# Rows transposed unscaled in the attention half, the inverse root moved behind the projection, and the side work placed at other ticks

## What is computed

```python
h = _layernorm(x) * (1 + ca) + sa
# for a in (global, local), with norm_w[a]:
hn = h * rsqrt(mean(h * h) + 1e-6) * norm_w[a]        # rmsnorm
q, k, v = split_heads(hn @ wq), ...                    # 16 heads of 8 for q, 4 for k and v
q, k = rope(q), rope(k)
q = q * rsqrt(mean(q * q) + 1e-6); k = ...             # qk_norm, per head
o = softmax(q @ k.T / sqrt(8), masked) @ v
h = h + merge_heads(o) @ wo
# then
x = x + ga * h
```

## Time and profile before

| | |
|---|---|
| median of 3 runs | 1370.69 us (1365.3 to 1371.41) |
| the profiled execution | 1370.85 us |
| its span | 1369.1 us |
| PE busy | 1176.2 us, 86% |
| DVE busy | 987.5 us, 72% |
| ACT busy | 821.8 us, 60% |
| POOL busy | 437.6 us, 32% |
| exponentials L742 | 384, 355.8 us |

### The profile page before, as it was taken

One profiled execution on the slowest core, in us unless ns is written; L12 is line 12 of the kernel. 1 busy time (PEld: TensorE's weight loads), 2 busy tenths in 40 slices (PEclk: granted clock), 3 DMA queues, 4 the chain that ended last, 5 costly groups with the idle time before them and its releaser, 6 DMA issues.

```text
span 1369.1 us, 36780 instructions
## 1 busy us (share of the span) xinstructions
PE 1176.2 (86%) x15602; PEld 698.9 (51%) x15602; DVE 987.5 (72%) x1573; ACT 821.8 (60%) x1218; POOL 437.6 (32%) x577
## 2 busy tenths in 40 slices
PE   3268888789888887867899999999999999999986
PEld 2123334344434554535566666666666666666653
DVE  4836765759575866869578777877778777877755
ACT  2179878788786664533555556455655566555641
POOL 1203030201013443665453333333433333333410
PEclk8579999999999998988899999999999999999997
DMA  3011302021021333110021011011110110111101
GB/s 97 5 38 44 124 29 85 18 92 32 17 94 32 125 109 109 48 45 18 17 76 26 21 26 26 21 25 26 29 26 22 25 26 22 27 24 26 29 6 62
DMA packets 37330, 59.79 MB, mean 44 GB/s; under 512 B 6416, under 2 KB 12464, under 8 KB 37168
## 3 DMA queue, kind: packets, MB, share of 16 engines
q1 hardware_dynamic: 37168, 57.44, 14.4%
HBM read 22.58 MB, written 16.78 MB: 29 GB/s over the span
## 4 chain that ended last, share of the span: by engine, by line
PE 46%; DVE 5%; issue 2%; ACT 1%; POOL 1%; DVEq 0%; POOLq 0%; ACTq 0%
PE psum L1229 8%; PE psum L1365 7%; PE psum L1318 5%; PE psum L1249 4%; PE psum L1340 4%; PE psum L1304 4%; PE psum L1239 4%; PE psum L1391 3%; DVE ffn_neg_max L1714 2%; PE psum L1289 1%; PE psum L1326 1%; PE psum L1295 1%; ACT ffn_hn L1570 1%; PE psum L1357 1%; PE psum L1261 1%
## 5 line engine op out<-in xcount | busy, mean ns | idle before, releaser
L742 ACT ACTIVATE att_probs<-psum 128x1024 f32<-128x1024 f32 (+2 forms) x384 | 355.8, 993 | 128.9 <-PE psum L586 127.3
L1661 POOL TENSOR_TENSOR ffn_rot<-ffn_rot,ffn_rot_sin 128x512 f32<-128x512 f32 x128 | 160.3, 1274 | 385.6 <-DVE ffn_rot L1692 385.6
L630 PE MATMUL psum<-att_probs,att_v 128*32 128x256 f32 (+3 forms) x3712 | 205.4, 349 | 2.2 <-DVE att_probs L905 1.3
L586 PE MATMUL psum<-att_q_stack,att_k_parts 64*128 64x512 bf16 (+4 forms) x1280 | 143.5, 299 | 43.6 <-ACT att_probs L742 28.6
L905 DVE TENSOR_TENSOR att_probs<-att_probs,att_causal_mask 128x1024 f32<-128x1024 f32 (+1 forms) x80 | 85.0, 1066 | 87.9 <-ACT att_probs L742 87.9
L630 PEld LDWEIGHTS psum<-att_probs,att_v 128*32 128x32 f32 x3712 | 97.0, 112 | 69.3 <-issue 40.5
L586 PEld LDWEIGHTS psum<-att_q_stack,att_k_parts 64*128 64x128 bf16 x1280 | 44.3, 95 | 146.4 <-ACT att_probs L742 88.6
L1543 ACT ACTIVATE ffn_max_t<-psum 68x128 bf16<-68x128 bf16 x64 | 17.4, 273 | 152.2 <-PE psum L1277 152.0
L1550 ACT ACTIVATE ffn_probs<-psum 128x1024 f32<-128x1024 f32 x64 | 65.6, 1025 | 59.2 <-PE psum L1304 59.2
L1512 ACT ACTIVATE ffn_sq<-psum 128x512 f32<-128x512 f32 x128 | 75.3, 594 | 27.9 <-PE psum L1229 27.7
L489 POOL TENSOR_TENSOR att_probs<-att_probs,att_local_mask 128x480 f32<-128x480 f32 (+1 forms) x48 | 61.9, 1295 | 79.9 <-ACT att_probs L742 79.8
(11 more groups left out here) (217 smaller groups left out, 2497.0 us busy)
## 6 DMA issues: line engine op xcount, KB each, us to landing
ffn_v_back<-ffn_v SPq DMA_DIRECT2D x120, 130.0 KB, 2.4
att_q_stack<-q_rows SPq DMA_DIRECT2D x28, 512.0 KB, 3.6
q_rows<-att_q_high SPq DMA_DIRECT2D x21, 256.0 KB, 4.5
q_rows<-att_q_mid SPq DMA_DIRECT2D x21, 256.0 KB, 4.2
q_rows<-att_q_low SPq DMA_DIRECT2D x14, 256.0 KB, 4.2
xres<-in_hidden SPq DMA_DIRECT2D x4, 512.0 KB, 4.3
out<-ffn_qk_t SPq DMA_DIRECT2D x3, 512.0 KB, 3.2
att_q_stack<-att_q_high SPq DMA_DIRECT2D x24, 32.0 KB, 2.0
```

Of the source, the lines that this page charges most:

```text
L586: ins = T.matmul(psum[:, banks[i] + at:banks[i] + at + width], k_parts[rows, p % 3, j, kt * P:(kt + 1) * P], q_stack[rows, turn % 2, j, q0 ...
L630: ins = T.matmul(psum[32 * g:32 * g + V_PAD, (4 + cc) * BANK + lo - cc * BANK: (4 + cc) * BANK + hi - cc * BANK], v[:, p % 4, kt, g, shift ...
L742: act.activation(probs[:, n % E_BUFS, 2 * j:2 * j + 2, 0:width], ps2((step % 2) * 2).rearrange("p (h c) -> p h c", h=2)[:, :, 0:width], AC ...
L1661: steps.did(pool.tensor_tensor(out, out, halves(k.rot_sin[:, n % 2, :])[:, :, 1 - half, :], ALU.add), g["added"] if half else None)
```

## The change

The rows are transposed as they are, and no longer wait for their inverse root; `scale` is gone. As q and k are normalised per head afterwards, an unscaled row changes only the weight of the epsilon: the head's epsilon becomes `eps_row`, the row's mean square (with its epsilon) times 1e-6. The values alone are multiplied by the inverse root, by DVE in the new steps `scale0` and `scale1`, which replace ACT's value copies. `refine` is the Newton step of the root alone. The tables of steps are shorter, there is one more (`CLOSE`, for phase 6), and nearly all ticks are other ones.

```diff
-LN_AT = (-14, -8, 10, 36)
-QKV_AT = (-10, -1, 25, 50, 75, 100, 125, 153)
-OUT_AT = ((23, 44, 47, 50), (70, 75, 94, 97), (100, 118, 120, 122), (144, 147, 149, 151),
-          (165, 167, 169, 176), (178, 180, 182, 184), (186, 190, 192, 194))
-POST_AT = (177, 186)
+LN_AT = (-14, -5, 19, 24)
+QKV_AT = (-12, 8, 34, 60, 85, 110, 135, 158)
+OUT_AT = ((23, 41, 63, 67), (72, 88, 92, 97), (100, 113, 117, 121), (129, 147, 149, 151),
+          (164, 166, 173, 175), (177, 179, 181, 183), (185, 189, 191, 193))
+POST_AT = (176, 184)
...
-RELAXED = dict(square=0, reduce=3, roots=6, scale=7, transpose=10, evacuate=11, project0=13, copy0=14, project1=16, copy1=17,
-               head_square=17, cos=18, head_reduce=20, head_roots=22, sin=21, newton=22, add=22, rotate=26, k_split=27,
-               q_transpose=29, q_hi=30, q_lo=31, k_transpose=33, k_hi=34, k_lo=34)
...
+RELAXED = dict(square=0, transpose=1, evacuate=2, reduce=3, roots=4, refine=4, project0=5, copy0=6, scale0=7,
+               project1=9, copy1=10, scale1=11, head_square=10, cos=11, head_reduce=13, sin=14, head_roots=14, newton=14,
+               add=15, rotate=18, k_split=19, q_transpose=21, q_hi=22, q_lo=23, k_transpose=24, k_hi=25, k_lo=25)
+FIRST = dict(square=0, transpose=0, reduce=0, evacuate=1, roots=1, refine=1, project0=2, project1=2, copy0=3, scale0=3,
+             copy1=3, scale1=3, head_square=3, cos=3, head_reduce=3, head_roots=4, sin=4, add=4, newton=4, rotate=4,
+             q_transpose=5, q_hi=5, k_split=5, q_lo=6, k_transpose=6, k_hi=6, k_lo=6)
+CLOSE = dict(square=0, transpose=1, evacuate=2, reduce=3, roots=4, refine=4, project0=4, copy0=5, scale0=6,
+             project1=7, copy1=8, scale1=9, head_square=8, cos=9, head_reduce=11, sin=12, head_roots=12, newton=12,
+             add=13, rotate=16, k_split=17, q_transpose=18, q_hi=19, q_lo=20, k_transpose=21, k_hi=22, k_lo=22)
+LAST = dict(square=0, transpose=0, evacuate=1, reduce=1, roots=2, refine=2, project0=2, copy0=2, scale0=3,
+            project1=4, copy1=4, scale1=5, head_square=4, cos=5, head_reduce=5, sin=6, head_roots=6, add=7, newton=7,
+            rotate=8, k_split=8, q_transpose=10, q_hi=11, q_lo=12, k_transpose=13, k_hi=14, k_lo=14)
...
-MODULATE_AT = -8
+MODULATE_AT = -10
...
                         if share[1]:
                             wait_side_free("transpose", p)
-                            pe.wait_ge(xr_ready, p + 1)
-                        transposes(side, nrm, share, xrt_in_psum)
+                            if a == 0:
+                                pe.wait_ge(h_ready, b + 1)
+                            else:
+                                pe.wait_ge(h_added, PHASES.index((0, b)) + 1)
+                        transposes(side, h[:, b], share, ht_in_psum)
...
                         c.did(act.activation(qk[:, tiles], src[:, :, 0:QK_COLS], ACT.Copy), qk_copied)
-                        c.did(act.activation(v_dims[:, p % 4, tiles],
-                                             src[:, :, QK_COLS:QKV_COLS].rearrange("p t (g d) -> p t g d", g=KV_HEADS),
-                                             ACT.Copy), v_ready)
...
+                for i in range(2):
+                    for p in qkv_due(("scale0", "scale1")[i], n):
+                        tiles = slice(i * TILES // 2, (i + 1) * TILES // 2)
+                        src = side_of(p, ("project0", "project1")[i]).rearrange("p (t c) -> p t c", t=TILES // 2)
+                        dve.wait_ge(qk_copied, 2 * p + i + 1)
+                        if p >= 4 and i == 0:
+                            dve.wait_ge(pv_done, last_unit[GROUP * (p - 4) + GROUP - 1] + 1)
+                        c.did(V.tensor_tensor(v_dims[:, p % 4, tiles],
+                                              src[:, :, QK_COLS:QKV_COLS].rearrange("p t (g d) -> p t g d", g=KV_HEADS),
+                                              widen(rstd[:, tiles].rearrange("p (t o u) -> p t o u", o=1, u=1),
+                                                    [P, TILES // 2, KV_HEADS, HEAD_DIM]), ALU.mult), v_ready)
...
                     c.did(V.tensor_scalar(row_sq[:], row_sq[:], 1.0 / D, ATT_EPS, ALU.mult, ALU.add), row_sq_ready)
-                for p in qkv_due("scale", n):
-                    a, b = PHASES[p]
+                    c.settle()
+                    c.did(V.tensor_scalar(eps_row[:], row_sq[:], ATT_EPS, None, ALU.mult))
+                for p in qkv_due("refine", n):
                     refine_root(row_turn["qkv", p])
-                    c.did(V.tensor_tensor(nrm[:], h[:, b], widen(rstd[:].rearrange("p (t o) -> p t o", o=1), [P, TILES, D]),
-                                          ALU.mult), xr_ready)
...
-                    c.did(V.tensor_scalar(mean_sq[:], mean_sq[:], 1.0 / HEAD_DIM, ATT_EPS, ALU.mult, ALU.add), mean_sq_ready)
+                    c.did(V.scalar_tensor_tensor(mean_sq[:], mean_sq[:], 1.0 / HEAD_DIM,
+                                                 widen(eps_row[:].rearrange("p (t o) -> p t o", o=1), [P, TILES, QK_HEADS]),
+                                                 ALU.mult, ALU.add), mean_sq_ready)
```

More of the change, by code:

```diff
@@ L247 @@
-FIRST = dict(square=0, reduce=0, roots=1, scale=1, transpose=2, evacuate=2, project0=3, copy0=3, project1=3, copy1=3,
-             head_square=4, cos=4, head_reduce=4, sin=5, add=5, head_roots=5, newton=5, rotate=5, k_split=5,
-             q_transpose=6, q_hi=6, q_lo=6, k_transpose=6, k_hi=6, k_lo=6)
-LAST = dict(square=0, reduce=1, roots=2, scale=3, transpose=7, evacuate=8, project0=9, copy0=9, project1=11, copy1=11,
-            head_square=11, cos=12, head_reduce=12, sin=13, add=14, head_roots=14, newton=15, rotate=16, k_split=16,
-            q_transpose=18, q_hi=19, q_lo=20, k_transpose=21, k_hi=22, k_lo=22)
@@ L254 @@
+LAST = dict(square=0, transpose=0, evacuate=1, reduce=1, roots=2, refine=2, project0=2, copy0=2, scale0=3,
+            project1=4, copy1=4, scale1=5, head_square=4, cos=5, head_reduce=5, sin=6, head_roots=6, add=7, newton=7,
+            rotate=8, k_split=8, q_transpose=10, q_hi=11, q_lo=12, k_transpose=13, k_hi=14, k_lo=14)
+QKV_STEPS = (FIRST,) + (RELAXED,) * (len(PHASES) - 3) + (CLOSE, LAST)
 URGENT = (0, len(PHASES) - 1)
@@ L336, in attention_stream @@
     mean_sq, root, rnorm, refine = (sb(n, [P, TILES, QK_HEADS]) for n in ("mean_sq", "root", "rnorm", "refine"))
+    eps_row = sb("eps_row", [P, TILES])
     stats, mv, mod = tail.stats, tail.mv, tail.mod
@@ L351, in attention_stream @@
     normed, h_ready, h_added = sem("normed"), sem("h_ready"), sem("h_added")
-    sq_ready, xr_ready, xrt_in_psum, ht_ready = sem("sq_ready"), sem("xr_ready"), sem("xrt_in_psum"), sem("ht_ready")
+    sq_ready, ht_in_psum, ht_ready = sem("sq_ready"), sem("ht_in_psum"), sem("ht_ready")
     qkv_in_psum, qk_copied, v_ready = sem("qkv_in_psum"), sem("qk_copied"), sem("v_ready")
@@ L498, in _ @@
                     if p not in URGENT:
-                        pool.wait_ge(xrt_in_psum, p)
+                        pool.wait_ge(row_sq_ready, row_turn["qkv", p - 1] + 1)
                         if a == 0:
@@ L646, in _ @@
                         share = share_of(qkv_tick(p, "transpose"), n, j, TILES)
+                        a, b = PHASES[p]
                         if share[1]:
                             wait_side_free("transpose", p)
-                            pe.wait_ge(xr_ready, p + 1)
-                        transposes(side, nrm, share, xrt_in_psum)
+                            if a == 0:
[3 more added lines that the diff above has]
+                        transposes(side, h[:, b], share, ht_in_psum)
                     for i in range(2):
@@ L756, in _ @@
                         if p:
-                            act.wait_ge(xrt_in_psum, p)
+                            act.wait_ge(row_sq_ready, row_turn["qkv", p - 1] + 1)
                         if a == 0:
@@ L770, in _ @@
                             act.wait_ge(head_sq_ready, p)
-                        if p >= 4 and i == 0:
-                            act.wait_ge(pv_done, last_unit[GROUP * (p - 4) + GROUP - 1] + 1)
                         c.did(act.activation(qk[:, tiles], src[:, :, 0:QK_COLS], ACT.Copy), qk_copied)
-                        c.did(act.activation(v_dims[:, p % 4, tiles],
-                                             src[:, :, QK_COLS:QKV_COLS].rearrange("p t (g d) -> p t g d", g=KV_HEADS),
-                                             ACT.Copy), v_ready)
                 for p in qkv_due("head_square", n):
@@ L860, in _ @@
                         dve.wait_ge(kt_in_psum, p)
-                    dve.wait_ge(xrt_in_psum, p + 1)
+                    dve.wait_ge(ht_in_psum, p + 1)
                     for i in range(2):
```

3 lines of the change are left out of this document (removed).

## The result

The changed kernel takes 1381.13 us in the median of four runs (1380.42 to 1381.33), the kernel before 1369.6 beside it. The ratio is 1.0079, with a 95% interval of 1.006 to 1.0098: slower by 0.8%, where 1366 was forecast. The profiled spans are 1379.3 and 1369.1 us.

The account below looks back on a forecast made before the run. ACT (84%) and PE (85%) were taken as near the bound in the global units. From 1370.85 us, start -14.1, waits going -20.1, waits coming +37.1, local units -6 and end -1.5 gave -4.6: 1366, range 1350 to 1384.

Parts of the forecast that it names:

- The start: Before the first score: transposes follow h directly, first score at 61.3 us, 14.1 us earlier, bounds 10 to 16.
- Phase 1: Ticks 19 to 31: layernorms of batches 2 and 3 moved into phase 1's DVE chain; waits of +15 us, bounds 6 and 20.
- piled up: Rival: head-root waits cost 4.5 us each, phase 1 its upper 20, POOL stands against DVE, small waits bite fully: 1385; chance 0.21.
- Waits that go: PE waits at ticks 50 and 75 and smaller ones at 35, 97, 118 to 122 vanish: -20.1 us with the value copies.
- (2) head roots: Phases 2, 3, 4: head_roots one tick after head_reduce, reduction ends 2.0, 2.3 and 2.0 us late: +6.3 us.
- (3) OUT 3 at 129: open0 moved from tick 144 to 129, q_transpose at 131 waits for its DVE step: 3.8 us of PE, +6.3 with clock.
- (4): k_transpose of phase 2 waits: +2.5 us.
- (5): PE side steps in scale0/scale1 ticks or one tick behind what they need: 0.8 to 2 us each, half of 14 counted, +7.
- The local units: Local units: some waits at 147 and 155 go, 3 us come at 153, q_transpose of phase 7 waits 7: net -6, bounds -14, +5.
- The end: Behind the local units: close and wo of OUT 6 one tick earlier, -1.5 us.
- The slack swallows it: Rival: ticks with side work already have ACT gaps, small waits cost nothing, phase 1 costs 9 us: 1353; chance 0.32.
- the start gives half: Rival: the start's chain is held by something the order doesn't show, 7 us of the gain are kept: 1373; chance 0.10.

Follow-up runs that it names:

- flow_old_ticks: The new flow of data alone, with every tick of the kernel before; 1365.63 us, ratio 0.9962 to the kernel before.
- best2: Against start_new_rest_old: last step of output projection 0 at tick 68 instead of 50, second of projection 1 at 76 instead of 75; 1348.60 us.
- best3: Against best2: second step of output projection 1 at tick 87 instead of 76; 1347.27 us, ratio 0.9829 to the kernel before.
- outs_spaced: Changed kernel with output projections 0 to 3 three ticks apart from each other and from QKV projections and transposes, instead of two; 1365.86 us.
- local_back: Changed kernel with the local units' layout of the kernel before (last QKV phase, last three output projections, two steps behind them); 1380.29 us.
- start_new_rest_old: Against flow_old_ticks: the changed kernel's start (first LN, QKV of phase 0, modulation), all other ticks old; 1350.68 us, ratio 0.985.

## Why the prediction was wrong, point by point

**The start**: -14.1 said, -15.6 found, and flow_old_ticks splits it into 2.8 for the flow and 12.8 for the places. Right. **Phase 1**: +15 said, bounds 6 and 20; +16.4 found. ACT's wait at tick 22 was to be 3.9 and is 3.46; batch 3's statistics were to come 1.5 late for their roots and come 3.86 late; PE's wait for the mask of tick 28 was to be 2.8 and is 5.89. The two last are larger since the four DVE rows of the pile took 10.97 us and not the 4.2 of their medians. I had this mechanism in the paragraph on the 1.77 us of the earlier trace rows, and in the rival "piled up" with +5, but not in the sum. That the term came out near the mark all the same is partly luck: the first wait was put too high, at 6.4 us with the clock, where unit 22 grew by 4.2, from 1.81 to 5.99.

The rule named there, the Trainium skill, "SBUF — State Buffer", section "Who interferes with whom", has an operation with both inputs in SBUF wait for a GpSimd instruction that reads SBUF; by that rule, the trace agrees, in three of the four phase 1 rows (the cast has one input), at 235.01 of best2 and at 234.70 of best3.

**Waits that go**, 20.1: units 50 and 75 fell from 9.63 and 9.78 us to 3.22 and 1.81. Right in the two main terms.

**(2) head roots**: the waits are 2.26, 2.75 and 2.08 us where 2.0, 2.3 and 2.0 were said; taking them away gave 8.8 us of window, not 6.3. **(3) OUT 3 at 129**: PE's 3.8 is 4.42, and unit 131 grew by 6.1, 6.3 said; with the 2.01 at 129 itself, which I had nowhere, moving the step back gave 8.3 us. POOL's square ahead of both wasn't in the term, so the agreement in size is partly luck. **(4)** 1.89 us of PE, unit 58 3.4 us longer, 2.5 said. These three are right in place and mechanism, (2) and (4) too small by a quarter.

**(5), the first step that failed.** "Behind waits 1 to 3 DVE has caught up, so I count half: +7." The places were right: 41, 65, 67, 90, 92, 117 and 121 all show longer units than in the kernel before, 14.5 us in all (41 only 0.4). The halving was wrong. Outs_spaced took the output steps out of these ticks and got 10.2 us back beyond OUT 3's, net of the waits that it added in five units; the seven units alone became 16.3 us shorter. So (5) in full is the 14 that I had written as the upper case, or a little more. DVE had caught up, but that isn't what these waits hang on: the PE step waits for one particular instruction, and a DVE that is idle beforehand doesn't make it start earlier. Before the row at 230.88 DVE is idle until 223.06 and again 0.61 us until 227.40; the two copies that PE waits for are queued behind a reduction of 1.21 us and start at 229.54. At 41, 67 and 121 DVE is even idle while PE waits, as the instruction that both need is ACT's copy.

**The local units, the second step that failed**: -6 said (bounds -14 and +5), +1.3 found, and 0 measured by itself with local_back, -1.5 us for the old layout in the units and +1.6 behind them. The waits that were named are there: 7 us for phase 7's query transposes is 5.94, 3 us at 153 is 2.96, and unit 155 and 147 are 7.0 us shorter. What came besides was put at nothing: ACT's 4.39 us at the head roots of phase 7, one tick behind their reduction as in (2), and PE's 4.08 us at 601.73, in the last unit. How much of the difference each of them makes wasn't measured.

With (5) in full and the local units at 0 the sum is -4.6 + 7 + 6 = +8.4 us, where +10.2 was measured. Either of the two corrections alone leaves it within 2.5 us of nothing.

**The end**: -1.5 said. The layout is worth 1.2 to 2.3 there at equal clock (below), the rest of the -5.1 goes with the clock of the two traced executions.

**The rivals.** "The slack swallows it" falls with outs_spaced; "the start gives half" with start_new_rest_old. "Piled up" named 1385 with (5) in full and POOL against DVE, and both are there; its price for the head roots, 4.5 us in each phase, is not: 8.8 for three. So the time lies between the sum and that rival, nearer to the rival. What I chose wrongly was the discount: the count by ticks gave each of these waits, no row spoke for its absorption, and I took half of it off.

Of the new instructions' prices, the value copy on DVE was put at 0.3 us, and the operation with the new epsilon at 0.1 over the 0.244 of the earlier trace rows, at most 0.2 over it. Groups of the changed kernel, 60 to 604 us:

```profile
L875 DVE TENSOR_TENSOR att_v<-psum,tail_rstd 128x128 f32<-128x128 f32 x14 | 4.0, 288 | 15.5 <-ACT att_qk L779 15.5
L961 DVE SCALAR_TENSOR_TENSOR att_mean_sq<-att_mean_sq,att_eps_row 128x160 f32<-128x160 f32 x7 | 3.0, 435 | 0.2
```

The first is 0.288; the second 0.435 in the mean, 0.33 in phases 2 to 4: its upper bound, on seven instructions, worth nothing in the sum.

## What to carry to other kernels

Where two engines are near their bound in a loop, as here at 84% and 85%, count a wait of one microsecond like one of six: in full, and look for the one instruction that releases it and the queue that this one stands in, not for the mean load around it. Ask two changes that come together for their price apart: here the data flow and the new start gave 20.5 us (ratio 0.985), and the new places of everything else took 31 back. Here the steps on the shared banks did better three ticks from their neighbours than two, and an output step one or two ticks ahead of the query transposes, where a long DVE chain is queued, cost a wait of 4.4 to 4.9 us both times.
